# One flamingo block on one core: opening and first group of the shared experts reordered, the summary added by VectorE, fills and small loads moved

## What is computed

```python
# third step, L1_xattn: a summary row per batch, added before a layernorm
proj = einsum('btd,ed->bte', states, W_out) + b_out
summary = mean(proj, axis=1, keepdims=True)
y = Z + summary                                  # Z = layernorm(x)
x = x + tanh(g) * ((y - mean(y)) / sqrt(var(y) + eps) * gamma + beta)

# fourth step, L1_ffn
flat = layernorm(x).reshape(N, D)
scores = softmax(flat @ Wr + router_bias)        # 64 experts, the best 4 of each token
eid, w = top_k(scores, 4)                        # weights are rescaled to sum to 1
pos = (cumsum(oh, 0) * oh).sum(-1) - 1           # place in the expert's buffer, 128 places
out = sum over k of w_k * expert[eid_k](flat)    # silu(x Wg) * (x Wu) @ Wd
out = out + sum_s (silu(flat Sg_s) * (flat Su_s)) @ Sd_s     # 2 shared experts, width 512
```

## Time and profile before

| | before |
|---|---|
| median of 3 runs | 1168.92 us (1167.15 to 1171.07) |
| the profiled execution | 1168.85 us |
| its span | 1167.1 us, 18338 instructions |
| PE busy | 1048.2 us (90%) |
| DVE busy | 656.2 us (56%) |
| POOL busy | 556.3 us (48%) |
| ACT busy | 480.6 us (41%) |
| `middle` in the span | begins at about 554 us |

### The profile page before, as it was taken

The page is one execution under the profiler, slowest core; times in us unless marked ns, Lnnn a source line. Parts: engine busy times, 40 slices in busy tenths (PEclk is TensorE's granted clock), DMA queues, the critical chain, the costliest instruction groups (busy, mean ns, idle before and its releaser), DMA issues. The chain is left out here.

```text
span 1167.1 us, 18338 instructions
## 1 busy us (share of the span) xinstructions
PE 1048.2 (90%) x5324; PEld 735.4 (63%) x5324; DVE 656.2 (56%) x1527; ACT 480.6 (41%) x835; POOL 556.3 (48%) x521
## 2 busy tenths in 40 slices
PE   3999999999879999998788799999999999999930
PEld 2555555655427777775288568577587777788820
DVE  4677787776448888886576526446231333344420
...
DMA packets 128138, 199.19 MB, mean 171 GB/s; under 512 B 35991, under 2 KB 44183, under 8 KB 128074
## 3 DMA queue, kind: packets, MB, share of 16 engines
...
q10 hardware_dynamic: 288, 0.52, 0.1%
...
## 5 line engine op out<-in xcount | busy, mean ns | idle before, releaser
L906 POOL TENSOR_TENSOR m_down_lo<-wo,m_down_hi 128x512 fp32r<-128x512 f32 x80 | 133.2, 1684 | 79.4 <-ACT m_down_hi L1001 79.4
L514 PE MATMUL bank<-win,vT 128*128 128x512 f32 x256 | 124.1, 598 | 0.0
L604 ACT ACTIVATE win<-bank 128x512 f32<-128x512 f32 x128 | 69.5, 595 | 110.5 <-PE bank L506 110.3
L674 DVE TENSOR_REDUCE negmax<-bank 128x1 bf16<-128x512 f32 x128 | 86.9, 679 | 43.5 <-PE bank L521 43.2
L1015 DVE TENSOR_TENSOR m_up_lo<-w,m_up_hi 128x1024 fp32r<-128x1024 f32 x80 | 98.3, 1229 | 12.1 <-ACT m_up_hi L973 11.0
L521 PE MATMUL bank<-k_hi,q_parts 128*128 128x512 f32 x128 | 76.9, 601 | 16.8 <-DVE negmax L674 13.4
L1235 POOL DMA_INDIRECT tab<-stage_up,slot x64 | 66.3, 1036 | 49.1 <-DVE slot L1570 30.9
L1972 PE MATMUL bank<-y,m_w 128*128 128x128 f32 x736 | 89.7, 275 | 0.0
L1942 POOL DMA_INDIRECT out<-m_y,m_token x32 | 49.6, 1550 | 80.8 <-DMA out<-m_y,m_token 42.7
L1972 PEld LDWEIGHTS bank<-y,m_w 128*128 128x128 f32 x736 | 86.4, 193 | 0.5 <-issue 0.5
L2088 PE MATMUL bank<-w_sd,stage_gate 128*128 128x512 f32 x192 | 85.8, 603 | 0.3 <-DVE stage_gate L2078 0.3
...
## 6 DMA issues: line engine op xcount, KB each, us to landing
...
```

Source lines behind the costliest of these rows:

```text
L514: nc.tensor.matmul(pO[s * 2 + h][:], vT[:, s, sb_, h:h + 2, :].rearrange("p a c -> p (a c)"), probs[:, sb_ % 2, h, :], start=(sb_ == 0), s ...
L604: nc.scalar.activation(probs[:, b % 2, h, :], pS[h][:], ACT.Exp, scale=1.0 / HEAD).then_inc(p_ready, 1)
L674: nc.vector.tensor_reduce(negmax[:, s, m:m + 1], pM[:], AX.X, ALU.max, negate=True).then_inc(pm_read, 1)
L906: nc.gpsimd.tensor_tensor(dn_lo[:, m, :], row(wo0, e * MB + m), dn_hi[:, m, :], ALU.subtract).then_inc(dn_lo_ready, 1)
```

## The change

- **TensorE, opening:** `mixed(0)` goes ahead of the first summary row; `with_beta(0)` and `with_beta(1)` go ahead of `mixed(2)`. The wait for the small loads covers two loads, not five.
- **TensorE, end of group 0:** all four transposes of the next group stand behind the third tile's down product, and all four logits behind the fourth (before: spread over the last three tiles).
- **VectorE, group 0:** `split(3)` moves to behind `product(0, 1)`; products 2 and 3 go inside `take_in(2)`; in the second half `choose` and `mark` come first, and the steps of the third step stand between the products. `normed` is gone: `made` computes z = x * rstd + summary in one instruction for each tile, without subtracting the mean (the next norm removes it).
- **ScalarE:** no longer applies the norm (L1485, 4 instructions in each of three groups); the second gate weight's high half is cast behind the first two `turn`s; the last two summary rows are copied behind the first gate cast.
- **GpSimd:** no longer adds the summary (L1246); the power of the last norm moves from ahead of `keep_low` to between the dispatches in group 0 and behind them in the others. The fills of `tokens`, the tail of `stage_all`, `power` and `chosen` move to the head of `mixture0`.
- **SyncE:** beta and gamma are loaded behind the second gather, ahead of the two gate weights; the router's weight and bias behind them.

The diff, cut to its core:

```diff
@@ GpSimd, head of mixture0 @@
+            nc.gpsimd.iota(T["tokens1"][:], [[P, TILES]], base=0, channel_multiplier=1)
+            nc.gpsimd.memset(T["stage_all"][:, NSH * DB * HSH:], 0.0)
+            nc.gpsimd.memset(T["power1"][:], -0.5)
+            nc.gpsimd.memset(T["chosen1"][:], 0.0)
@@ GpSimd, middle @@
-            nc.gpsimd.iota(tokens[:], [[P, TILES]], base=0, channel_multiplier=1)
-            nc.gpsimd.memset(T["stage_all"][:, NSH * DB * HSH:], 0.0)
-            nc.gpsimd.memset(power[:], -0.5)
-            nc.gpsimd.memset(chosen[:], 0.0)
-            pool.drain()
...
                 for j in range(TPB):
-                    if n == 1 and j == 0:
-                        pool.wait_ge(summary_ready, B)
-                    pool.wait_ge(z_ready, (n - 1) * TPB + j + 1)
-                    nc.gpsimd.tensor_tensor(z[:, j, :], z[:, j, :], summary[:, n, :], ALU.add).then_inc(y_ready, 1)
-                for j in range(TPB):
+                    pool.wait_ge(y_ready, (n - 1) * TPB + j + 1)
                     nc.gpsimd.tensor_tensor(x_sb[:, n * TPB + j, :], x_sb[:, n * TPB + j, :], beta[:],
                                             ALU.add).then_inc(xb_ready, 1)
...
-            sum_up(1)
-            dispatch(0, range(TPB))
-            keep_low(1)
-            for n in range(2, B):
-                gather(n, range(TPB))
-                dispatch(n - 1, (0, 1))
+            for n in range(1, B):
+                if n > 1:
+                    gather(n, range(TPB))
+                    dispatch(n - 1, (0, 1))
                 sum_up(n)
-                dispatch(n - 1, (2, 3))
+                if n == 1:
+                    dispatch(0, (0, 1))
+                    inverse_std(stat(0, 2))
+                    dispatch(0, (2, 3))
+                else:
+                    dispatch(n - 1, (2, 3))
+                    inverse_std(stat(n - 1, 2))
                 keep_low(n)
@@ TensorE @@
             def first_steps():
+                mixed(0)
                 summary_row(0)
-                mixed(0)
                 mixed(1)
                 summary_row(1)
+                with_beta(0)
+                with_beta(1)
                 mixed(2)
                 summary_row(2)
                 summary_row(3)
-                with_beta(0)
-                with_beta(1)
                 mixed(3)
-                pe.wait_ge(small_loaded, 80)
+                pe.wait_ge(small_loaded, 32)
...
+                if g == 0:
+                    between = ((), (), ((transposed, 0), (transposed, 1), (transposed, 2), (transposed, 3)),
+                               tuple((logit, j) for j in range(TPB)))
@@ ScalarE @@
-            summary_rows(range(B))
+            summary_rows(range(2))
             act.wait_ge(gate_loaded, 16 * NSH)
-            first_part(SPLITS[NSH:])
+            first_part(SPLITS[NSH:NSH + 1])
+            summary_rows(range(2, B))
...
             for j in range(2):
                 turn(0, j)
+            first_part(SPLITS[NSH + 1:])
@@ VectorE: the steps of a norm @@
-            dve.wait_ge(small_loaded, 80)
+            dve.wait_ge(bout_loaded, 16)
             dve.wait_ge(s_full, 1)
             nc.vector.tensor_tensor(srow, pL[0:B, :], bout, ALU.add).then_inc(srow_ready, 1)
-            nc.vector.tensor_scalar(beta[:], beta[:], gates[:, 1:2], None, ALU.mult).then_inc(beta_ready, 1)
+
+            def scale_beta():
+
+                dve.wait_ge(affine_loaded, 32)
+                nc.vector.tensor_scalar(beta[:], beta[:], gates[:, 1:2], None, ALU.mult).then_inc(beta_ready, 1)
...
+            def made(g):
+
+                rooted(stat(g, 0))
+                if g == 0:
+                    dve.wait_ge(summary_ready, B)
+                else:
+                    dve.wait_ge(fT_kept, TPB * (g + 1))
+                for j in range(TPB):
+                    t = (g + 1) * TPB + j
+                    nc.vector.scalar_tensor_tensor(z[:, j, :], row(x_sb, t), rstd[:, j:j + 1], summary[:, g + 1, :],
+                                                   ALU.mult, ALU.add).then_inc(y_ready, 1)
...
@@ VectorE: first_step @@
                 mix_in(2)
-                split(3)
                 product(0, 0)
                 attend_to(2)
                 product(0, 1)
+                split(3)
                 take_in(2)
-                product(0, 2)
                 combine(0, 0)
-                product(0, 3)
+                product(0, 4)
                 combine(0, 1)
-                product(0, 4)
+                product(0, 5)
                 combine(0, 2)
-                product(0, 5)
...
-                normed(0)
+                measure()
+                choose(0)
                 product(0, 0, 1)
-                choose(0)
+                mark(0)
                 product(0, 1, 1)
-                mark(0)
+                made(0)
                 product(0, 2, 1)
+                summed(0)
+                product(0, 3, 1)
                 find(0)
-                product(0, 3, 1)
+                product(0, 4, 1)
                 place(0)
-                product(0, 4, 1)
-                summed(0)
+                attend(0)
                 product(0, 5, 1)
-                attend(0)
+                attended(0)
                 product(0, 6, 1)
-                attended(0)
+                settled(0)
                 product(0, 7, 1)
                 flattened(0)
@@ VectorE: step(g) for g = 1, 2 @@
-                            normed(g)
+                            measure()
+                            made(g)
+                        if n == 4:
+                            summed(g)
                         if n == 5:
-                            summed(g)
+                            attend(g)
                         if n == 6:
-                            attend(g)
                             attended(g)
+                            settled(g)
@@ SyncE @@
-            sp.dma_start(bout, A["L1_xattn_b_out"].partition_broadcast(B)).then_inc(small_loaded, 16)
-            sp.dma_start(gamma[:], A["L1_xattn_gamma"].partition_broadcast(P)).then_inc(small_loaded, 16)
-            sp.dma_start(beta[:], A["L1_xattn_beta"].partition_broadcast(P)).then_inc(small_loaded, 16)
-            sp.dma_start(wr[:], A["L1_ffn_Wr"].rearrange("(b p) e -> p b e", p=P)).then_inc(small_loaded, 16)
-            sp.dma_start(bias_r[:], A["L1_ffn_router_bias"].partition_broadcast(P)).then_inc(small_loaded, 16)
+            sp.dma_start(bout, A["L1_xattn_b_out"].partition_broadcast(B)).then_inc(bout_loaded, 16)
             sp.wait_ge(gathered[1], 16 * 2)
+            sp.dma_start(beta[:], A["L1_xattn_beta"].partition_broadcast(P)).then_inc(affine_loaded, 16)
+            sp.dma_start(gamma[:], A["L1_xattn_gamma"].partition_broadcast(P)).then_inc(affine_loaded, 16)
...
+            sp.dma_start(wr[:], A["L1_ffn_Wr"].rearrange("(b p) e -> p b e", p=P)).then_inc(small_loaded, 16)
+            sp.dma_start(bias_r[:], A["L1_ffn_router_bias"].partition_broadcast(P)).then_inc(small_loaded, 16)
```

66 lines of the change are left out of this document (34 added, 32 removed).

## The result

| | before | after |
|---|---|---|
| median, timed together | 1168.98 us (4 runs, 1167.15 to 1171.07) | 1150.12 us (4 runs, 1147.57 to 1154.12) |
| the profiled execution | 1168.85 us | 1147.57 us |
| its span | 1167.1 us | 1145.9 us |

The ratio on record is 0.9857, with a 95% interval from 0.9828 to 0.9886. By it the time is 16.7 us less (13.3 to 20.1 by the interval); the two medians differ by 18.9 us. Timed a second time, on another occasion, the changed kernel took 1151.45 us (4 runs, 1149.07 to 1154.26) against 1166.89 us (7 runs), a ratio of 0.9873 (0.9836 to 0.9910), where the medians differ by 15.4 us. The forecast was 1153.5 us, in a range of 1149.5 to 1159.5.

What follows compares the result with a forecast made beforehand. TensorE (PE) was taken to set the time until the expert block's DMAs. Its terms brought group 1's first chunk to 677.0 instead of 692.38, so 1168.85 - 15.4 = 1153.5 us, range 1149.5 to 1159.5.

Steps and rivals of the forecast that it cites:

- The whole: Start of shared experts to group 1's first chunk: 15.4 us less, carried to the end, 1153.5 us.
- signs of being wrong: `made` instructions over 1.5 us each, chunk 8 later than 618, or group 1's first chunk to end off 475 by over 2.
- The opening: Start of `middle`: betas moved ahead let VectorE take tiles in earlier; 2.2 us, bounds 0.5 and 2.9.
- rival 2: Opening gives nothing: beta and gamma land late, VectorE waits until 571, the 2.2 us are lost, 1155.7 us; chance 0.10.
- The wait ahead of chunk 4: Group 0, first half: product 2 inside `take_in(2)` removes TensorE's 1.43 us wait; chunk 8 starts at 615.8.
- The wait for the mask: Group 0, behind chunk 10: choice without GpSimd's adds beside it removes 4.38 us, and 2.3 more as the clock stays up.
- Late next, chunk 15: Group 0, second half: TensorE waits for product 13, 0.6 us plus 1.3 for GpSimd's adds beside `made`; down products at 642.4.
- rival 1: Second half, group 0: port taken in turns, `made` costs 2.6 us more, clock falls; 3.6 us, 1157.1 us; chance 0.20.
- the higher level through chunks 11 to 15: Group 0, second half: expected sign that TensorE's clock stays at its higher level through these chunks, the mask wait gone.
- The end of group 0: `flat` ready before TensorE, 6.09 us wait gone, transposes 3.2 us; group 1's first chunk at 677.0 instead of 692.38.
- Groups 1 and 2: `made` adds VectorE 2.8 us, up to 5.4, in each, but TensorE doesn't wait: 0 us.
- rival 4: Expert block is bound by its DMAs and gives the gain back; time stays at 1169 us; chance 0.05.

Runs made afterwards that it cites:

- second profile: Changed kernel, nothing edited, profiled once more: 1149.07 us; the kernel before was also profiled again, 1167.39 us.
- experiment 2: Changed kernel with TensorE's opening order, the fills, or the small loads each put back alone: 32.52, 30.36 and 31.01 us from start of `middle` to first chunk.
- old_products: Changed kernel with TensorE's opening products in the order of the kernel before: 32.52 us from start of `middle` to first chunk, against a median of 30.13.
- experiment 3: Changed kernel with the router's choice put back late (mask 9.1 us behind chunk 8), or with five extra GpSimd adds beside it (7.84 us).

## Why the prediction was right, point by point

- *The whole.* 15.4 us by the sum; 15.0 and 15.8 us in the two pairs of profiles, from the start of `middle` to group 1's first chunk; 18.9 and 15.4 us between the medians of the two sets of timings, 16.7 and 14.8 by their ratios. Part of the closeness is luck: in the first pair the opening gave 0.8 us more than the sum had, the way from the first chunk to the down products 1.5 less, and the rest 0.3 more. The difference between 1150.12 and 1153.5 is no larger than what executions of one kernel differ by; 4.05 us ahead of `middle` and 2.12 us in the tail of the first pair weren't the change's. The last distance, foreseen as 475 within 2, was 472.6, just outside, so one of my signs of being wrong came up; the second profile has 475.17, and TensorE's part of the distance is unchanged in both.
- *The opening*: 2.2 us, with 2.9 as the upper bound. It gave 2.8 (median of nine profiles; 1.9 to 3.0). The reason held: VectorE's wait of 2.90 us for the betas is gone, and VectorE reached the step ahead of the take-in at the time that it had before (experiment 2). My term was too small because I had laid TensorE's steps end to end with the lengths of before, partly at the lower clock: from the third mix to the fourth I had 6.3 us, and it took 5.4 (4.6 in the second profile). No run puts the place of the betas back and nothing else; old_products was spoilt by the clock. The gate weights took 11.5 us to land where I had 10, and ScalarE waited for them, but nothing depended on it. Beta and gamma landed in 3.9 and 5.8 us. So rival 2 didn't happen in its full size, but VectorE waited 0.62 us for gamma here, and up to 1.67 in other profiles: the move was not free with time to spare, as I had written.
- *The wait ahead of chunk 4* went, and chunk 8 came 30.70 us behind the first chunk (29.68 in the second profile), where the sum had 31.0.
- *The wait for the mask* went, and my reason was the larger part of it but not all. I put it down to GpSimd's adds alone; they have 4.1 of the 7.0 us, about the 4.3 that I had, and the place of the choice in the list has 2.9. The place alone makes a wait of only 0.31 us for the mask, but costs 2.05 us at the down products (experiment 3).
- *Late next, chunk 15.* The place was right. `made` lost 2.0 us to the adds where I had taken 1.3 (bounds 0 and 2.6), the waits were 0.45 and 2.34 us instead of 1.9, and behind the longer one the clock fell, 1.2 us, which I had priced only in rival 1; the sign "the higher level through chunks 11 to 15" did not hold. The down products came 59.14 us behind the first chunk (58.13 in the second profile), not 57.6. So rival 1 came about in part, for some 2 us of its 3.6. I had let the clock fall only behind a wait of over 3 us; here it fell behind one of 2.34 us.
- *The end of group 0*: `flat` ready ahead of TensorE, 3.2 us for the transposes (3.3 measured, 659.64 to 662.94), 34.6 us from the down products to group 1's first chunk (34.3 measured, 639.04 to 673.30). `lnf` came at 654.57, 74.7 us behind the first chunk; I had 659 - 584.8 = 74.2. This stretch is half of the gain, and no run puts its order on TensorE back alone. By the rows, `lnf` comes 7.9 us earlier than before (74.67 against 82.58), and TensorE reaches the transposes one tile, 7.0 us, later behind the down products. With the old order it would stand there at 59.14 + 13.97 = 73.1, and `flat` would be there at 74.67 + 1.14 = 75.8 (1.14 us from `lnf` to the transpose before): some 2.7 us of the 6.09 us wait would be left, an estimate.
- *Groups 1 and 2*: nothing, 199.8 us before and after to the start of `experts`. `made` ran there beside nothing that TensorE waits for, and PE's only wait behind group 0 is still the 1.8 us at the block's border. The expert block moved along in full, 226.6 us to its last matmul both times: rival 4 has no support in any profile.
